# Four-layer transformer on one core: folding, normalising and summing moved in the last attention, token choice layer reordered

## The reference

```
x = layernorm(x + windowed attention(x))        # 16 heads, window 128
x = layernorm(x + token choice experts(x))      # groups of 16 tokens, 64 experts
x = layernorm(x + linear attention(x))
x = layernorm(x + nested-width attention(x))
```

```
q, k, v = projections of the first 256, 128, 64, 32 columns, for the four quarters of the tokens
attn = softmax(q k^T * scale)                   # full, over all tokens, 8 heads
out = (attn v) o_w + o_b, again in nested widths, + x
```

## Time and profile before

| | value |
|---|---|
| median of 3 runs | 2693.75 us |
| the profiled execution's own time | 2702.53 us |
| its span | 2700.7 us |
| mean granted TensorE clock | 0.931 |
| PE busy | 2229.6 us, 83% |
| DVE busy | 1432.7 us, 53% |
| ACT busy | 963.6 us, 36% |
| POOL busy | 823.6 us, 30% |

### The profile page before, as it was taken

One profiled execution on the slowest core, in us unless ns is written; L12 is line 12 of the kernel. 1 busy time (PEld: TensorE's weight loads), 2 busy tenths in 40 slices (PEclk: granted clock), 3 DMA queues, 4 the chain that ended last, 5 costly groups with the idle time before them and its releaser, 6 DMA issues. The chain is left out here.

```text
span 2700.7 us, 43328 instructions
## 1 busy us (share of the span) xinstructions
PE 2229.6 (83%) x17584; PEld 1404.6 (52%) x17584; DVE 1432.7 (53%) x2566; ACT 963.6 (36%) x1385; POOL 823.6 (30%) x469
## 2 busy tenths in 40 slices
PE   2899999999999997677877489998388888888884
PEld 1445555555554554565656346666255555555552
DVE  1445555555555553444545415554367776677672
ACT  0233333333333332543444133332144444444441
POOL 4122121111222210112122111110235665566566
PEclk7899999999999998888989789999589999999997
DMA  6545456565545441577467531100553354335411
GB/s 134 115 96 118 103 111 116 112 117 119 103 103 126 95 80 34 193 241 253 172 243 251 181 109 63 63 32 0 175 144 105 100 164 127 111 100 164 112 40 47
DMA packets 226534, 328.99 MB, mean 122 GB/s; under 512 B 14384, under 2 KB 164128, under 8 KB 226080
## 3 DMA queue, kind: packets, MB, share of 16 engines
q1 hardware_dynamic: 223520, 325.56, 45.6%
q10 hardware_dynamic: 2816, 0.65, 0.2%
HBM read 197.59 MB, written 127.93 MB: 121 GB/s over the span
## 5 line engine op out<-in xcount | busy, mean ns | idle before, releaser
L461 ACT ACTIVATE l0a_probs<-l0a_slot 128x1024 f32<-128x1024 f32 (+1 forms) x256 | 248.4, 971 | 337.9 <-PE l0a_slot L621 189.1
L1574 POOL TENSOR_TENSOR l1f_added<-l1f_probs 128x1024 f32<-128x1024 f32 x120 | 281.4, 2367 | 278.6 <-ACT l1f_probs L1630 278.4
L1630 ACT ACTIVATE l1f_probs<-l1f_slot 128x1024 f32<-128x1024 f32 x240 | 244.5, 1022 | 335.2 <-PE l1f_slot L1805 325.7
L518 DVE TENSOR_REDUCE l0a_rowmax<-l0a_slot 128x4 f32<-128x1024 f32 (+1 forms) x256 | 293.4, 1156 | 130.0 <-PE l0a_slot L631 127.1
L1684 DVE TENSOR_REDUCE l1f_rowmax<-l1f_slot 128x1 f32<-128x1024 f32 x240 | 287.4, 1217 | 62.0 <-PE l1f_slot L1796 61.5
L1805 PE MATMUL l1f_slot<-l1f_Qs,l1f_Ks 128*128 128x256 f32 x960 | 172.8, 304 | 52.7 <-DVE l1f_rowmax L1684 26.4
L421 POOL TENSOR_TENSOR l0a_turned<-l0a_turned 128x512 f32<-128x512 f32 x32 | 40.7, 1273 | 560.7 <-DVE l0a_turned L504 560.7
L1796 PE MATMUL l1f_slot<-l1f_Ks,l1f_Qs 96*128 96x512 f32 x480 | 176.9, 454 | 31.5 <-DVE l1f_rowmax L1684 21.3
L1805 PEld LDWEIGHTS l1f_slot<-l1f_Qs,l1f_Ks 128*128 128x128 f32 x960 | 144.5, 195 | 108.5 <-DVE l1f_rowmax L1684 46.5
L621 PE MATMUL l0a_slot<-l0a_mask,l0a_ident 128*128 128x512 bf16 (+1 forms) x512 | 150.6, 377 | 25.8 <-issue 23.5
L563 PE MATMUL l0a_O<-l0a_probs,l0a_V 128*32 128x128 f32 x3840 | 156.7, 279 | 11.7 <-issue 11.7
(11 more groups left out here) (189 smaller groups left out, 3985.0 us busy)
## 6 DMA issues: line engine op xcount, KB each, us to landing
expert_outputs<-l0f_wide SPq DMA_DIRECT2D x64, 512.0 KB, 4.0
l0f_wide<-expert_outputs SPq DMA_DIRECT2D x32, 1024.0 KB, 9.4
l0a_Qs<-qk_rows SPq DMA_DIRECT2D x96, 256.0 KB, 7.6
l0a_Ks<-qk_rows SPq DMA_DIRECT2D x96, 256.0 KB, 14.7
l1f_Ks<-kq_rows SPq DMA_DIRECT2D x48, 512.0 KB, 8.0
l0f_f<-in_dram SPq DMA_DIRECT2D x10, 2048.0 KB, 15.6
qk_rows<-l0a_hi SPq DMA_DIRECT2D x32, 512.0 KB, 2.8
qk_rows<-l0a_lo SPq DMA_DIRECT2D x32, 512.0 KB, 4.2
```

The source lines that it names most:

```text
L461: exp_ready.by(act.activation(probs[:, t % 2, HG * g:HG * g + HG, 0:reach, :], s[:, :, 0:reach, :], ACT.Exp, scale=SCALE))
L518: max_ready.by(dve.reduce_max(rowmax[:, t, :, 2 * g:2 * g + 2], s[:, :, :, first:2 * P], AX))
L1574: add_done.by(pool.tensor_tensor(added[:, u, :], probs[:, 0, u, :], probs[:, 1, u, :], ALU.add))
L1630: exp_done.by(act.activation(probs[:, half, u - FIRST[b], :], s[:, :], ACT.Exp, scale=SCALE))
```

## The change

Four things change.

1. In all LayerNorms the addition of the epsilon moves from DVE to POOL, right ahead of the power.
2. In the last attention POOL folds the probabilities twice: after the addition of the halves (128x1024) it adds the upper half of the result to the lower one, in place (128x512), with a wait for its own first addition between them (`halved`). The matmuls of ones go over two slices instead of four. ACT's exponentials wait for `halved` alone. For the last batch of the last sequence POOL adds nothing, and PE sums all eight slices of `probs`.
3. In the last attention the own LayerNorm's result is applied by ACT instead of POOL, in the same steps. POOL computes the negated product `own_shift` in step rescale 0, and ACT waits for it.
4. The token choice layer's list is reordered, and `lo` gets a semaphore for each half. The first `lo` of the layer goes to DVE. In the last pass POOL rescales 2 tiles instead of 8 and DVE the other 14.

```diff
@@ LayerNorm: aggregate (DVE), reciprocal_root (POOL)
-        dve.wait_ge(self.aggregated, n * self.tiles)
-        dve.tensor_scalar(self.mv[:, :, 1], self.mv[:, :, 1], LN_EPS, None, ALU.add).then_inc(self.var_ready, 1)
+        pool.wait_ge(self.aggregated, self.count(b, use) * self.tiles)
+        pool.tensor_scalar(self.mv[:, :, 1], self.mv[:, :, 1], LN_EPS, None, ALU.add).then_inc(self.var_ready, 1)
@@ token choice layer: steps
-    steps = [(-1, "gather", 1), (0, "f2", 0)] + s[:10] + merged(s[10:], late) + [(0, "spread", 1)]
-    steps += e[:4] + [(-1, "aggregate", 0)] + e[4:] + [(0, "gather", 0)]
+    turned = selection(1)[:2]
+    steps = [(-1, "gather", 1), (0, "f2", 0)] + s[2:11] + merged(s[11:], late[:3]) + [late[3], (0, "spread", 1)]
+    steps += e[:1] + [(-1, "aggregate", 0)] + e[1:5] + [(-1, "rescale", 0), e[5], (-1, "rescale", 1), e[6], (-1, "rescale", 2), e[7],
+                                                        (-1, "rescale", 3), turned[0], e[8], turned[1], e[9]]
+    steps += [(-1, "store", 1), (-1, "store", 0), (0, "gather", 0), (1, "load", 0), (1, "load", 1), (0, "f2", 1)]
-    steps += merged(s[:10], [(-1, "rescale", n) for n in range(4)] + [(-1, "store", 0), (-1, "store", 1), (1, "load", 0), (1, "load", 1), (0, "f2", 1)])
-    steps += merged(s[10:], early[:2]) + [(1, "xT", 0), (1, "xT", 1), early[2], (1, "xT", 2), (1, "xT", 3), (1, "logits", 0), early[3]]
-    steps += [(1, "spread", 0)] + e[:4] + [(1, "second", 0)] + e[4:6] + [(1, "hi", 0), (1, "lo", 0)] + e[6:8] + [(1, "hi", 1), (1, "lo", 1)] + e[8:]
+    steps += s[2:14] + merged(s[14:], early[:1]) + [early[1], (1, "xT", 0), (1, "xT", 1), early[2], (1, "xT", 2), (1, "xT", 3), early[3]]
+    steps += [(1, "logits", 0), (1, "spread", 0)] + e[:4] + [(1, "second", 0)] + e[4:6] + [(1, "hi", 0), (1, "lo", 0)] + e[6:8]
+    steps += [(1, "hi", 1), (1, "lo", 1), (1, "pT", 0), e[8], (1, "pT", 1), e[9]]
@@ token choice layer: POOL, DVE
-                    rescale(pool, X, 0, range(NT))
+                    rescale(pool, X, range(NT) if X + 1 < NB else range(2))
-                    rescale(dve, X, 1, range(NT + 2 * i, NT + 2 * i + 2))
+                    rescale(dve, X, range(NT + 2 * i, NT + 2 * i + 2) if X + 1 < NB else ((2, 3, 4), (5, 6, 7), (8, 9, 10, 11), (12, 13, 14, 15))[i])
+                if kind == "lo" and X == 0 and i == 0:
+                    low(dve, X, 0)
@@ last attention: POOL
-                if kind == "add":
+                if kind == "add" and not at_end(X, OF_UNIT[i]):
-                    add_done.by(pool.tensor_tensor(added[:, u, :], probs[:, 0, u, :], probs[:, 1, u, :], ALU.add))
+                    halved.by(pool.tensor_tensor(added[:, u, :], probs[:, 0, u, :], probs[:, 1, u, :], ALU.add))
+                    halved.wait(pool, X, i + 1)
+                    add_done.by(pool.tensor_tensor(added[:, u, 0:SKT * QW], added[:, u, 0:SKT * QW], added[:, u, SKT * QW:HKT * QW], ALU.add))
                 if kind == "rescale":
                     if i == 0:
                         own_ln.reciprocal_root(pool, X, 0)
-                    own_ln.normalise(pool, total, total, X, 0, (2 * i, 2 * i + 1))
+                        negative_mean(own_ln, own_shift, own_shifted, X)
@@ last attention: ACT
+            def normalise(ln, by, ready, part, X, tiles):
+                wait_alone(act, ready, X + 1)
+                for t in tiles:
+                    act.activation(part[:, t, :], part[:, t, :], ACT.Identity, bias=by[:, t:t + 1], scale=ln.rstd[:, t:t + 1]).then_inc(ln.normed, 1)
+                if kind == "rescale":
+                    normalise(own_ln, own_shift, own_shifted[1], total, X, (2 * i, 2 * i + 1))
-                    add_done.wait(act, X if b else X - 1, behind)
+                    halved.wait(act, X if b else X - 1, behind)
@@ last attention: PE
-                    add_done.wait(pe, X, FIRST[i] + units)
-                    for j in range(HKT):
+                    if at_end(X, i):
+                        parts = [probs[:, half, 0:units, QW * j:QW * j + QW] for half in range(2) for j in range(HKT)]
+                    else:
+                        add_done.wait(pe, X, FIRST[i] + units)
+                        parts = [added[:, 0:units, QW * j:QW * j + QW] for j in range(SKT)]
```

More of the change, by code:

```diff
@@ L729, in token_choice_layer @@
         xT_even = signal("xT_even", CH); xT_odd = signal("xT_odd", CH)
-        hi_ready = signal("hi_ready", 2); lo_ready = signal("lo_ready", 2)
+        hi_ready = signal("hi_ready", 2); lo_ready = [signal(f"lo_ready{n}", 1) for n in range(2)]
         rated = signal("rated", 2); best_ready = signal("best_ready", 2); choice_ready = signal("choice_ready", 2)
@@ L757, in hidden_free, with low, rescale @@
             schedule.wait_filled(eng, X if p >= 8 else X - 1, ("inter", (p - 8) // 2 % (2 * IN)))
-        def rescale(eng, X, n, tiles):
+        def low(eng, X, n):
+            part = slice(NT * n, NT * n + NT)
+            hi_ready.wait(eng, X, n + 1)
+            lo_ready[n].by(eng.tensor_tensor(lo[:, part, :], x[:, X % 2, part, :], words(hi[:, part, :]), ALU.subtract))
+        def rescale(eng, X, tiles):
             wait_alone(eng, ln.rstd_ready, ln.count(X, 0))
             for t in tiles:
-                normed[n].by(eng.tensor_scalar(x[:, X % 2, t, :], x[:, X % 2, t, :], ln.mv[:, t, 0:1], ln.rstd[:, t:t + 1],
+                normed[t // NT].by(eng.tensor_scalar(x[:, X % 2, t, :], x[:, X % 2, t, :], ln.mv[:, t, 0:1], ln.rstd[:, t:t + 1],
                                                ALU.subtract, ALU.mult))
@@ L810, in _ @@
         def _(pool):
-            for s in (lo_ready, spread_ready[1], normed[0]):
+            for s in (lo_ready[1], spread_ready[1], normed[0]):
                 s.start(pool)
@@ L816, in piece @@
                 _, kind, i = step
-                if kind == "lo":
-                    part = slice(NT * i, NT * i + NT)
-                    hi_ready.wait(pool, X, i + 1)
-                    lo_ready.by(pool.tensor_tensor(lo[:, part, :], x[:, X % 2, part, :], words(hi[:, part, :]), ALU.subtract))
+                if kind == "lo" and (X or i):
+                    low(pool, X, i)
                 if (kind, i) == ("spread", 1):
@@ L824, in piece @@
                     alone(pool)
-                    lo_ready.wait(pool, X)
+                    for ready in lo_ready:
+                        ready.wait(pool, X)
                     for j in range(J):
@@ L898, in _ @@
         def _(dve):
-            for s in (xT_odd, rated, best_ready, choice_ready, normed[1], sel_odd, hidden_odd, inter_odd, summed):
+            for s in (xT_odd, rated, best_ready, choice_ready, lo_ready[0], normed[1], sel_odd, hidden_odd, inter_odd, summed):
                 s.start(dve)
@@ L953, in piece @@
                     if i == 0:
-                        lo_ready.wait(dve, X)
+                        for ready in lo_ready:
+                            ready.wait(dve, X)
                     if i >= NC:
@@ L989, in piece @@
                     if i < TP and i % (TP // 2) == 0:
-                        lo_ready.wait(pe, X, 2 * i // TP + 1)
+                        lo_ready[2 * i // TP].wait(pe, X)
                 if kind == "h" and i % 2 == 0:
@@ L1471, in nested_width_attention_layer, with at_end @@
         schedule.signals(filled, reader)
+        def at_end(X, b):
+            return X == NSEQ - 1 and b == NB - 1
         NCONST = 11
```

33 lines of the change are left out of this document (17 added, 16 removed).

## The result

The changed kernel took 2714.26 us, the median of five runs (2710.81 to 2722.14), beside 2693.75 of the kernel before (2693.16 to 2701.06): 1.0072 of its time, 95% interval 1.0051 to 1.0093, or some 20 us slower. The two profiled executions differ by less, 2712.4 to 2700.7 in span, because that of before lay 8.8 above its median and that of after at its median; a comparison by stages has to be read with that in mind.

What follows compares the result with a forecast made beforehand. PE was taken to bound the last attention. Its +27 us, −19 for the token choice layer and +0.5 elsewhere sum to +8.5 on the median 2693.75, giving 2703 us, with an 8-in-10 range of 2679 to 2728.

Steps and rivals of the forecast that it cites:

- The sums: Last attention: folding twice halves PE's sums of 1.91 us, −0.95 each, −24 us together.
- The tail: End of the last attention's last sequence: later PE work and a longer last sum against a shorter own result, +2 us together.
- ACT behind POOL in row 4: Last attention, row 4: ACT waits for POOL's own_shift behind lengthened additions, so PE's nat29 comes later; +33 us over six sequences.
- Rows 5 to 7: Last attention: lengthened additions delay the first LayerNorm's shift, which ACT's normalise 0 in row 6 awaits; +7 us over six sequences.
- The epsilon: Epsilon on POOL: adds some 0.15 us at a layer's end, nothing inside, where PE is the bound; +0.5 us.
- The token choice layer: Reordered token choice layer as a whole: its terms together shorten it, −19 us.
- (c): Token choice layer: stores ahead of the gather let the loads land some 5 us earlier in two passes, −10 us.
- (d): Token choice layer: logits behind out3 no longer hide ACT's spread, +2 us in each of three passes, +6.
- (f): Token choice layer, last pass: 14 tiles on DVE take 6.0 us against POOL's 9.90 for eight, −3.9 us.
- (b): Token choice layer: DVE's last sel copy comes sooner, removing the 2.79 us wait of the experts' first matmuls; −8 over three passes.
- Rival (A): Last attention: ACT's wait is hidden, so the added costs there fall away, 2645 us; chance 0.16.
- Rival (B): Token choice layer gains nothing, as DVE's tiles beside POOL's take 1.24 us instead of 0.43; 2722 us, chance 0.16.

## Why the prediction was right, and where two of its terms were wrong

The direction, the place and the mechanism were as forecast; the time, 2714, lies 11 above 2703 and inside the range. Point by point:

**The sums, −24.** 827.3 to 803.0, −24.3, in which the tail's net is contained. One sum went from 1.91 to 1.05, so −0.86 and not −0.95. **The tail, +2:** from the first sum of the last sequence to the end it is 80.7 before and 80.4 after, with the halved sums in it.

**ACT behind POOL in row 4, +33, its clock, +9, and the like in the last sequence, +8.3.** Shown: the pair 3.69, the wait 5.96 against 6.0, 8.05 in the last sequence, and 48.1 for the seven blocks (after against rescale in row 5), 10.0 of it PE's busy time, where the sum had 50.

**Rows 5 to 7, +7.** This is the term that was mis-sized: it measured 26.7. The step that failed is the comparison of the new chain (21.8) with the spacing of before (20.58), and it failed twice. First, the exponential at 2140.17 is that of tr27. The one that stands behind `normalise` 0, and whose slot PE takes next, is tr26's:

```profile
2134.62 1.08 ACT L1593 ACTIVATE l1f_xn<-l1f_xn,l1f_shift,l1f_first_rstd 128x256 f32<-128x256 f32 x2
2135.84 1.02 ACT L1630 ACTIVATE l1f_probs<-l1f_slot 128x1024 f32<-128x1024 f32 x1
```

```profile
2138.94 0.71 PE L1796 MATMUL l1f_slot<-l1f_Ks,l1f_Qs 96*128 96x512 f32 x2
```

PE took the slot at 2138.94, 19.35 behind the start at 2119.59. Second, the spacing of before held a whole sum and the wait in DVE's epsilon, which other edits of the same change take away. It was 19.3 to 23.8 in the six sequences of before, is 18.2 to 18.9 with the epsilon alone moved, and 17.0 to 17.7 in the run with normalise in row 7, where nobody waits for the chain. The chain itself took 20.7, less than the 21.8 of the sum, so it comes some 3.4 late and not 1.2; the waits read 2.9 to 3.5, and behind some of them the clock is lost as well.

**The epsilon, +0.5.** Wrong in its premise, "inside, where PE is the bound". The row that I showed said 1.11 for DVE; I used it for the start of a chain and not as time in which DVE's next row maximum, and with it PE, stands still, twice in a sequence. Shown: −16.9 in the last stretch if it is the only edit (−7.8 of idle time, the rest with the clock), ratio 0.9964. But in the company of the others it is +17.0: there POOL's chain decides, to which the epsilon adds 0.5, and it ends the delay of the exponentials that had covered a part of that chain. One edit, both signs.

With both of them corrected my own sum would have been 8.5 + 20 (rows 5 to 7) − 17 (the epsilon alone), about +11, which is near the 11.7 of the two profiles: the two errors nearly cancelled, and the good hit of the total was partly luck. Against the 20 of the medians it leaves 9 unexplained, about as much as the profiled execution of before lay above its median. By runs, the last attention's stretch goes so: 827.3 (the epsilon in it) − 24.3 + 26.7 + 48.1 = 877.8. The steps are differences of neighbouring runs, so they must sum; each holds for the company in which it was made.

**The token choice layer, −19.** −21.3 by the two profiles; over ten profiles with the new order it is 499.7 to 507.1 long, in the two with the old one 528.4 and 535.7, so −21 to −36, and a difference under some 7 us between two profiles tells nothing. The terms: the loads (c) +14.4 when undone, of which 8.6 can be read at the loads, where the sum had 10; the logits (d) −7.1 when undone, no more than that spread, where it had 6; the last pass's tiles (f) −4.7 by the wait for the next layer's load, where it had −3.9. (b) held its place, the 2.79 became 0.64, but the wait for the gather behind it took most of it back (PE's first wait for it in that pass: 6.42 after 5.99), and a stretch that I had not looked at, the last pass's second half, became 7 shorter. Its cause was only read, from waits of 1.41 and 2.41 for DVE that stood there before and are gone.

**Rival (A)**, ACT's wait hidden at 2645, is near what the kernel becomes when the steps are moved, though not for a reason that (A) gave: with rescale in row 5 it took 2663.5, with normalise in row 7 as well 2636. **Rival (B)**, DVE and POOL taking turns, fell: 0.37 for a tile on DVE beside POOL. The Trainium skill's "SBUF — State Buffer" (section "SBUF: two separate sides") calls the shared port pair of the two engines an exclusive lock, held for a whole instruction; but it limits it to VectorE instructions in a two-port mode, or with two inputs in SBUF against a GpSimd instruction that reads SBUF, and my use of it for the tiles left that limit out. The rows agree with the lock for the 128x8 epsilon, which ends with POOL's addition each time. The tiles don't wait, and no row here shows in which mode either instruction ran.

What stays open: why the medians of the kernel before and its run with the epsilon moved differ by 10 us where the last stretch differs by 17, beyond the 7.3 by which the token choice layer differs in those two executions.

## What to carry to other kernels

Where several edits go in together, cost each one against the schedule that the others leave, not against the one in the trace: a chain that seemed 1.2 us late by the old spacing was some 3.4 late by the new one, and an operation of 0.2 us was worth −17 us where it freed the engine in demand and +17 where it lengthened the chain in demand. When an engine is given work that waits for another engine, look at what stands behind it in its own queue and move the step to where its input has long been ready: with the same instructions the kernel took 2714 us when they stood where the input was late, and 2636 when they stood a row later. And shortening a wait can be worth more than its length: with 5.96 us of idle time PE lost its clock, with 2.28 it did not.

## What the runs showed of the hardware

An addition of a constant to 128x8 values takes 0.17 us on DVE where POOL is idle beside it. Where POOL is in the middle of an addition it ends only with that, within 0.04 us, in 26 of 26 cases of two kernels, and takes 0.57 to 1.17; on POOL it takes 0.24. DVE's row maxima and aggregates beside the same additions are not slowed (1.22 and 0.15 either way). Normalising tiles of 128x256 on DVE, by a mean and a factor of each partition, doesn't wait for POOL doing the same (0.37 each in the middle passes; 0.43 at the end of the layer before).

After an idle time of 2.28 us PE's next matmuls ran at 0.73 for two (full clock), after 5.96 at 1.22 and with a granted clock of 0.50 for several microseconds; after 2.9 to 3.3 it was now the one (0.70), now the other (1.19).

The best kernel of the study is the changed one with rescale in row 5 and normalise in row 7: 0.9785 (0.9759 to 0.9811) of the time before, and 0.9755 (0.9724 to 0.9785) with the logits ahead of the last combination, which these runs can't tell apart.
